# A four-layer perceiver kernel on one core: layer 2's cross attention moved to float32r in two parts, and five joints reordered

## The reference

```python
x = x + _L2_xattn_ref(ctx_1024, _layernorm(x))   # softmax(h_dec @ h_enc^T) @ h_enc, one head, 256 features
x = x + _L2_attn_ref(_layernorm(x), ...)         # begins with rmsnorm(x, w), 16 heads of 64
x = x + _L1_ffn_ref(_layernorm(x), ...)          # 16 experts, top 2 by a gate, and a shared one
x = x + _L1_attn_ref(...)  # ... @ Wu + bu
x = x + _L3_attn_ref(...)  # ... @ Wout + bout
```

## Time and profile before

| | us |
|---|---|
| median of 3 runs (lowest, highest) | 2077.07 (2073.99, 2083.38) |
| profiled execution, time of the run | 2084.2 |
| its span, first to last instruction | 2082.9 |
| busy in the span: PE / weight loads | 1902.7 (91%) / 1193.7 |
| VectorE / ScalarE / Pool | 1357.7 (65%) / 1219.6 (59%) / 542.5 (26%) |
| chain that ended last: PE / VectorE / ScalarE | 67% / 21% / 7% |
| mean granted TensorE clock | 0.955 |

### The profile page before, as it was taken

The page is one execution under the profiler, slowest core; times in us unless marked ns, Lnnn a source line. Parts: engine busy times, 40 slices in busy tenths (PEclk is TensorE's granted clock), DMA queues, the critical chain, the costliest instruction groups (busy, mean ns, idle before and its releaser), DMA issues.

```text
span 2082.9 us, 36948 instructions
## 1 busy us (share of the span) xinstructions
PE 1902.7 (91%) x13683; PEld 1193.7 (57%) x13683; DVE 1357.7 (65%) x3230; ACT 1219.6 (59%) x2770; POOL 542.5 (26%) x697
## 2 busy tenths in 40 slices
PE   7999999998998899999999877898898799788998
PEld 4555555554565455555555556657556688564656
DVE  3776668883767577667796567531356898477383
ACT  3787778895435288778888452342155687164251
POOL 2111111122621111011100355200033466164151
PEclk9999999999999699999999788999999899999999
DMA  9777567760113677667761213333101242200110
GB/s 207 155 147 146 116 129 149 146 136 1 41 41 55 122 143 144 124 115 154 148 94 17 84 34 107 112 103 99 46 21 59 85 123 72 86 1 9 41 54 11
DMA packets 114225, 191.48 MB, mean 92 GB/s; under 512 B 17096, under 2 KB 67072, under 8 KB 107520
## 3 DMA queue, kind: packets, MB, share of 16 engines
q1 hardware_dynamic: 113056, 188.11, 41.2%
q10 hardware_dynamic: 992, 1.02, 0.2%
HBM read 135.20 MB, written 2.69 MB: 66 GB/s over the span
## 4 chain that ended last, share of the span: by engine, by line
PE 67%; DVE 21%; ACT 7%; issue 2%; DMA 1%; POOL 1%; SPq 0%; DVEq 0%; ACTq 0%; POOLq 0%
DVE WK L861 9%; PE PS L798 8%; PE PS L688 8%; PE PS L356 6%; PE PS L705 6%; PE PS L364 5%; PE PS L676 4%; PE PS L717 4%; PE PS L1886 3%; PE PS L1911 3%; PE PS L2319 3%; PE PS L465 2%; PE PS L2261 2%; PE PS L492 2%; PE PS L513 2%
## 5 line engine op out<-in xcount | busy, mean ns | idle before, releaser
L861 DVE TENSOR_REDUCE WK<-PS 128x1 f32<-128x1024 f32 x512 | 621.6, 1223 | 227.5 <-PE PS L688 163.1
L969 ACT ACTIVATE WK<-PS 128x512 f32<-128x512 f32 x840 | 464.5, 601 | 38.9 <-PE PS L688 24.4
L688 PEld LDWEIGHTS PS<-QSR,KSR 51*128 51x128 f32 x2048 | 251.5, 187 | 244.1 <-ACT WK L969 91.0
L688 PE MATMUL PS<-QSR,KSR 51*128 51x256 f32 x2048 | 379.5, 307 | 9.6 <-ACT WK L969 1.3
L676 PE MATMUL PS<-KSR,QSR 51*128 51x512 f32 x1024 | 371.4, 454 | 9.3 <-DVE WK L861 3.4
L798 PE MATMUL PS<-WK 128*32 128x256 f32 x2528 | 219.5, 394 | 0.6 <-ACT WK L953 0.5
L676 PEld LDWEIGHTS PS<-KSR,QSR 51*128 51x128 f32 x1024 | 186.4, 188 | 21.5 <-issue 13.4
L992 POOL TENSOR_TENSOR WK<-WK 128x512 fp32r<-128x512 f32 x62 | 79.3, 1279 | 442.5 <-ACT WK L930 230.7
L564 ACT ACTIVATE WK<-PS,WK 128x256 f32<-128x256 f32 (+1 forms) x320 | 140.6, 451 | 77.4 <-DVE WK L532 48.3
L590 POOL TENSOR_TENSOR WK<-WK 128x128 f32<-128x128 f32 (+1 forms) x128 | 64.9, 507 | 255.1 <-DVE WK L550 219.4
L594 POOL TENSOR_TENSOR WK<-WK 128x512 f32<-128x512 f32 x96 | 99.9, 1041 | 74.3 <-DVE WK L547 56.3
(11 more groups left out here) (360 smaller groups left out, 3548.0 us busy)
## 6 DMA issues: line engine op xcount, KB each, us to landing
KSR<-WK SPq DMA_DIRECT2D x381, 128.0 KB
WB<-in_ctxT SPq DMA_DIRECT2D x78, 512.0 KB, 5.0
WK<-in_ctxT SPq DMA_DIRECT2D x40, 512.0 KB, 4.1
WA<-in_ctxT SPq DMA_DIRECT2D x26, 512.0 KB, 5.2
WK<-in_ctx SPq DMA_DIRECT2D x8, 1024.0 KB, 6.0
WK<-in_ctx SPq DMA_DIRECT2D x16, 512.0 KB, 4.3
QSR<-scratch_q SPq DMA_DIRECT2D x48, 128.0 KB, 4.4
WB<-in_L3f_qkv SPq DMA_DIRECT2D x2, 1536.0 KB, 6.6
```

What stands on the lines that cost most here:

```text
L688: return pe.e.matmul(tile["S", L, s, i][:, j * 256:j * 256 + 256], KS[s % 4][HALF[i % 2], kt * 128:(kt + 1) * 128], QS[HALF[i % 2], g % 2, ...
L861: dv.e.tensor_reduce(mt[:, n:n + 1], tile["R", L, s, n].rearrange("p a b -> p (a b)"), AX, ALU.max).then_inc(*dv.at("R", L, s, n))
L969: ac.e.activation(PR[n % NPR], tile["S", L, s, i], ACT.Exp).then_inc(*ac.at("E", L, s, i))
```

## The change

**Layer 2's cross attention in float32r, two parts.** `ctxT` and `ctx` chunks come in units of 1024 columns, numbered `n` 0 to 31 (16 and 16). ScalarE rounds a unit into `CH2[n % 4]` (`high2_act`), Pool subtracts it from the unit in place (`low2_pool`), giving the low part (`CXR`). ScalarE rounds the two halves of the transposed input into `HH2`, and VectorE writes `HL2`. A score tile is 6 matmuls instead of 2 (float32 ones). In phase 2 ScalarE rounds all transposed blocks (`PH2`), VectorE writes the low part (`PL2`), and a block has 3 products. `expx` is in halves of 2048 columns: batch 0's stand between batch 1's chunks, and batch 1's between batch 0's steps. In batch 1, VectorE copies the scores of tile `q=1`. `CT2` has 5 buffers, `CN2` 6 of 512 rows. The first two units are rounded and subtracted at the end of layer 1. `rms_b` writes `XR` from `X` with a root of `var * (1 + eps) + 1e-5 * eps`, instead of statistics of `XN`.

**Joints.** The ranking of the experts is done for all four tiles at once, comparisons (`rank_compare`) ahead of expert 1 and the rest (`rank_weigh`) behind it. The two biases are added to `X` by Pool at the start of the self attention. `ln0b` takes its root from the variance directly, ahead of the other.

```diff
@@ l2x_pe
+                    h, l = view(CH2[n % 4], 0, 1024, 2, 512), view(low2(n), 0, 1024, 2, 512)
                     for q in range(2):
+                        m = slice((bb * 2 + q) * 128, (bb * 2 + q + 1) * 128)
+                        b = take(banks, ("s2", n, q), ((dv if bb and q else ac), "s2c", n, q))
                         settle(b)
+                        pe.wait_ge(ac, "c2h", n)
                         for k in range(2):
-                            i = pe.e.matmul(b.ap, HT[:, k, t * 128:(t + 1) * 128], CT2[n % 3][:, k, :], start=k == 0,
-                                            stop=k == 1)
+                            pe.e.matmul(b.ap, HH2[:, k, m], h[:, k, :], start=k == 0, stop=False)
+                            pe.e.matmul(b.ap, HL2[:, k, m], h[:, k, :], start=False, stop=False)
+                        pe.wait_ge(po, "c2l", n)
+                        for k in range(2):
+                            i = pe.e.matmul(b.ap, HH2[:, k, m], l[:, k, :], start=False, stop=k == 1)
...
+                                pe.e.matmul(y, PH2[n % 4][:, c], h[:, j, :], start=k == 0, stop=False)
+                                pe.e.matmul(y, PH2[n % 4][:, c], l[:, j, :], start=False, stop=False)
+                                i = pe.e.matmul(y, PL2[n % 4][:, c], h[:, j, :], start=False, stop=k == 31)
@@ new helpers
+        def high2_act(n):
+            a, sem, event = raw2(n)
+            ac.wait_ge(sem, event)
+            if n >= 20:
+                ac.wait_ge(pe, "c2", (n - 20) * 2 + 1)
+            elif n >= 4:
+                ac.wait_ge(pe, "s2", n - 4, 1)
+            ac.e.activation(CH2[n % 4], WK[:, a:a + 1024], ACT.Copy).then_inc(*ac.at("c2h", n))
...
+        def low2_pool(n):
+            a = raw2(n)[0]
+            po.wait_ge(ac, "c2h", n)
+            po.wait_ge(po)
+            po.e.tensor_tensor(low2(n), WK[:, a:a + 1024], CH2[n % 4].bitcast(F), ALU.subtract).then_inc(*po.at("c2l", n))
@@ l2x_act, phase 2
+                    for q in range(2):
+                        n = (bb * 8 + g) * 2 + q
+                        ac.wait_ge(pe, "p2", n, 3)
+                        if n >= 4:
+                            ac.wait_ge(pe, "c2", n - 4)
+                        ac.e.activation(PH2[n % 4], tile["p2", n], ACT.Copy).then_inc(*ac.at("p2", n))
+                    if bb * 8 + g + 19 < 32:
+                        high2_act(bb * 8 + g + 19)
+                    if bb == 0 and g in (1, 2, 4, 5):
+                        expx(1, g % 3 - 1, g // 3)
@@ l1f_dve
+                if i == 0:
+                    low_act(0)
+                    rank_compare()
+                if i == 1:
+                    low_act(1)
+                    rank_weigh()
@@ l1f_act, at its end
+            for n in range(2):
+                high2_act(n)
@@ l1a_pool
+            po.wait_ge(d_l1a)
+            for t in range(NT):
+                po.wait_ge(dv, ("a1", "ln"), t)
+                po.wait_ge(po)
+                po.e.tensor_tensor(X[:, t, :], X[:, t, :], bu, ALU.add).then_inc(*po.at("xb1"))
```

More of the change, by code:

```diff
@@ L228, in build @@
         d_exp = [dma(f"expert{i}") for i in range(11)]
-        d_ct2 = [dma(f"l2ct{i}") for i in range(3)]
-        d_cn2 = [dma(f"l2cn{i}") for i in range(3)]
+        d_ct2 = [dma(f"l2ct{i}") for i in range(5)]
+        d_cn2 = [dma(f"l2cn{i}") for i in range(6)]
         d_ct3 = [dma(f"l3ct{i}") for i in range(3)]
@@ L1744, in l1f_dve, with rank_compare @@
         def l1f_dve():
[L1745 to L1750 removed]
+            def rank_compare():
+                for t in range(NT):
+                    dv.wait_ge(ac, "gate", t)
                 dv.e.tensor_tensor(cmpA, gj, gi, ALU.is_equal).then_inc(*dv.at())
@@ L1849, in l1f_pool @@
             end(po, "l1f")
+            for n in range(2):
+                low2_pool(n)
         def l1f_sp():
@@ L1858, in l1f_sp @@
                 load_expert(i)
-            for n in range(3):
+            for n in range(5):
                 sp.e.dma_start(CT2[n], tiles(D["ctxT"][:, n * 512:(n + 1) * 512])).then_inc(*d_ct2[n].at(n))
-            for n in range(3):
-                sp.e.dma_start(CN2[n], tiles(D["ctx"][n * 1024:(n + 1) * 1024, :])).then_inc(*d_cn2[n].at(n))
+            for m in range(4):
+                load_cn2(m)
         S2 = [view(WK, 4096 * i, 4096) for i in range(4)]
-        CT2 = [view(WK, 16384 + 1024 * i, 1024, 2, 512) for i in range(3)]
@@ L1868, in build @@
-        CN2 = [view(WK, 19456 + 2048 * i, 2048, 8, 256) for i in range(3)]
-        PT2 = [view(WK, 25600 + 512 * i, 512) for i in range(4)]
-        mxs = WK[:, 27648:27712]
+        CT2 = [view(WK, a, 1024, 2, 512) for a in (16384, 17408, 18432, 23552, 24576)]
+        CN2 = [view(WK, 19456 + 1024 * i, 1024, 4, 256) for i in range(6)]
+        PH2 = [EAR[:, 512 * i:512 * i + 512] for i in range(4)]
+        PL2 = [EAR[:, 2048 + 512 * i:2560 + 512 * i] for i in range(4)]
+        HH2, HL2 = view(EAR, 4096, 1024, 2, 512), view(EAR, 5120, 1024, 2, 512)
@@ new lines, in build, with raw2, load_cn2, low2 @@
+        CH2 = [WAR[:, 1024 * i:1024 * i + 1024] for i in range(4)]
+        mxs = WK[:, 32768:32832]
+        def raw2(n):
+            if n < 16:
+                return (16384, 17408, 18432, 23552, 24576)[n % 5], d_ct2[n % 5], n
+            m = n - 16
+            return 19456 + m % 6 * 1024, d_cn2[m % 6], m
+        def load_cn2(m):
+            sp.e.dma_start(CN2[m % 6], tiles(D["ctx"][m * 512:(m + 1) * 512, :])).then_inc(*d_cn2[m % 6].at(m))
+        def low2(n):
+            a = raw2(n)[0] - 16384
+            return CXR[:, a:a + 1024]
@@ L1872, in l2x_pe @@
         def l2x_pe():
             after(pe, "l1f")
-            turn_pe("h2x", XN, (dv, "ln2x"), dv, ac)
-            pe.wait_ge(dv, "h2x", 0)
-            pe.wait_ge(ac, "h2x", 1)
+            for f in range(2):
+                b = take(banks, ("h2x", f), (dv, "h2x", f))
+                settle(b)
+                for t in range(NT):
+                    pe.wait_ge(dv, "ln2x", t)
+                    pe.e.transpose(b.ap[:, t * 128:(t + 1) * 128], XN[:, t, f * 128:(f + 1) * 128],
+                                   idf[:, :]).then_inc(*pe.at("h2x", "T", f, t))
@@ L1877, in l2x_pe @@
+            for f in range(2):
+                pe.wait_ge(dv, "h2x", f)
             for bb in range(2):
@@ L1922, in peak, with rms_b @@
                                        negate=True).then_inc(*dv.at("m2", bb, q))
+            def rms_b(t):
+                dv.wait_ge(ac, "rms2", "sd", t)
+                dv.e.reciprocal(rs[:, t:t + 1], rs[:, t:t + 1]).then_inc(*dv.at())
+                dv.wait_ge(dv)
+                dv.e.tensor_scalar(XR[:, t, :], X[:, t, :], mv[:, t, 0:1], rs[:, t:t + 1], ALU.subtract, ALU.mult).then_inc(
+                    *dv.at("rms2", t))
             after(dv, "l1f")
-            turn_dve("h2x", 0)
+            for f in range(2):
+                dv.wait_ge(ac, "h2x", "hi", f)
+                dv.e.tensor_tensor(HL2[:, f, :], tile["h2x", f], HH2[:, f, :].bitcast(F), ALU.subtract).then_inc(
+                    *dv.at("h2x", f))
             for bb in range(2):
@@ L1999, in l2x_sp @@
             sp.e.dma_start(sm[:, 8:10], D["L2a_w"]).then_inc(*d_l2a.at())
-            for n in range(3, 16):
-                sp.wait_ge(pe, "s2", n - 3, 1)
-                sp.e.dma_start(CT2[n % 3], tiles(D["ctxT"][:, n * 512:(n + 1) * 512])).then_inc(*d_ct2[n % 3].at(n))
-            for n in range(3, 8):
-                sp.wait_ge(pe, "c2", (2 * (n - 3) + 1) * 2 + 1)
-                sp.e.dma_start(CN2[n % 3], tiles(D["ctx"][n * 1024:(n + 1) * 1024, :])).then_inc(*d_cn2[n % 3].at(n))
+            for n in range(5, 16):
+                sp.wait_ge(pe, "s2", n - 5, 1)
+                sp.e.dma_start(CT2[n % 5], tiles(D["ctxT"][:, n * 512:(n + 1) * 512])).then_inc(*d_ct2[n % 5].at(n))
+            for m in range(4, 16):
+                if m < 6:
+                    sp.wait_ge(pe, "s2", m + 9, 1)
+                else:
+                    sp.wait_ge(pe, "c2", (m - 6) * 2 + 1)
+                load_cn2(m)
+        EPS2 = float(np.finfo(np.float32).eps)
         L2A, a0 = [], 0
@@ L2612, in l3a_pool @@
                                            ALU.mult).then_inc(*po.at("rope3", l))
+            po.wait_ge(d_l3a)
+            for t in range(NT):
+                po.wait_ge(dv, ("a3", "ln"), t)
+                po.wait_ge(po)
+                po.e.tensor_tensor(X[:, t, :], X[:, t, :], ob3, ALU.add).then_inc(*po.at("xb3"))
             attn_pool(A3)
```

196 lines of the change are left out of this document (88 added, 108 removed).

## The result

| | kernel before | changed kernel |
|---|---|---|
| median of the runs on one chip, us (lowest to highest) | 2080.23 (2073.99 to 2096.3) | 2052.36 (2048.77 to 2055.27) |
| ratio to before, with its 95% interval | | 0.9849 [0.9814, 0.9884] |
| span of the profiled execution | 2082.9 | 2047.4 |
| mean granted clock | 0.955 | 0.959 |

The changed kernel is faster, by about 1.5%. The profiled executions lie 35.5 us apart, where the sum of terms said 37.7. The same kernel was measured twice more: 2044.47 us, ratio 0.9825 [0.9779, 0.9871], span 2045.0; and 2046.99 us, 0.9817 [0.9775, 0.9859], span 2049.0.

A forecast was written before the change was run, and what follows sets the result against it. PE was taken to bound layer 2's cross attention, VectorE alone the joints; terms of 26.0 us inside the stage, -2.9, +4.0, +6, +2.0, +1.8 and +0.8 sum to 37.7, giving 2039 us, range 2026 to 2057.

The forecast's parts named there:

- Scores, 11.6: Layer 2's cross attention scores: 192 float32r instructions at 0.228 us, 45.6 us against 57.2, gain 11.6 us.
- Products and the joint of the batches, 14.4 in sum: Layer 2's products gain 9.3 us, less 2.0 for the first wait and 1.4 for slips; the batches' joint gains 8.5.
- The lock and the split input, -2.9: Start of layer 2's scores: a VectorE tensor_scalar waits out Pool's subtraction, 2.2 us; splitting the transposed input adds 0.7.
- End of the stage, 4.0: End of layer 2's cross attention: 7.25 us falls to 3.2, the second norm's variance coming from the first's; gain 4.0.
- Ranking, 6: Layer 1's experts: comparisons before expert 1, the rest behind it, shorten PE's idle; gain 6 us, bounds 4 and 10.
- Layer 1's end, 2.0: Layer 1's self attention: bias additions leave VectorE's chain, but Pool's splits catch the tensor_scalars; gain 2.0 us (0 to 4).
- Layer 3, 1.8: Layer 3: four bias additions of 0.42 us plus gaps leave VectorE's chain, Pool being free; gain 1.8 us.
- Layer 0, 0.8: Layer 0, root to first normalised tile: one root, two small products and a round trip less; gain 0.8 us.
- Lock everywhere: Rival: each joint waits out a whole Pool operation, ranking and bias gain 2 instead of 8; time 2051 us, 15%.
- ScalarE or Pool as the bound: Rival: ScalarE's roundings or Pool's subtractions, not PE, bound layer 2; time 2042 to 2047 us, say 2045, 15%.
- Fewer meetings: Rival: no lock at the start of layer 2, ranking gains 10, the batches' joint 9.5; time 2031 us, 10%.
- Lower clock level over the stage: Rival: layer 2 runs at 1.2 GHz, 105 us more if throughout; over half of it, 2092 us; 3%.

The follow-up runs named there:

- split_f32: The kernel before with only batch 1's exponentials halved inside batch 0's steps and their maxima found ahead, products left in float32: ratio 0.9934.
- low_late: The changed kernel with Pool's second subtraction for layer 2 waiting until VectorE has normalised the last tile: 2041.28 us, ratio 0.9813.
- rank_old: The changed kernel with the old ranking, tile by tile between the experts' elements: 2055.1 us, ratio 0.9836.
- all_late: The changed kernel with Pool's second layer 2 subtraction and its later expert operand splits waiting for VectorE's normalizations and ranking: 2039.27 us, ratio 0.976.
- r_after: The changed kernel measured and profiled once more, with no edit: 2044.47 us, ratio 0.9825.
- two_products: The changed kernel with the third product left out, except for one matmul per score tile: 2031.14 us, ratio 0.9761.
- exp_late: The changed kernel with batch 1's four half exponentials put back behind batch 0's steps: 2048.15 us, ratio 0.985.

## Why the prediction was right

The mechanism was right nearly everywhere. The total fell in the range with some luck: three medians, 2052, 2044 and 2047, all lie above 2039, and by the first alone the rival at 2051 would look better. What decides against that rival is the terms.

- **Scores, 11.6: measured 11.1.** The instruction of 512 columns was taken from the expert loop, and stood the same, 0.228. The 0.5 is the clock: 0.94 in the stage, 0.96 assumed.
- **Products and the joint of the batches, 14.4 in sum: measured 15.7.** By parts: the first batch gained 2.0 where 4.65 less 3.4 for the first wait and the slips was forecast, the second 5.0 where it was 4.65, the joint 8.75 (12.0 to 3.25) where it was 8.5. The first product waits 1.40 us, not 2.0. The mis-sized term was left out rather than wrong: that the idle of 12 us also cost 1.3 us of lower clock behind it, which split_f32 showed and the earlier trace rows had on its last line, 4.74 against 3.46. Without it the arithmetic gave the second batch 3.9 (33.1 in split_f32 to 29.2), not 4.65: here two misses partly cancel. The prediction also named ScalarE alone as the cause of the joint, and the description of the kernel before has the maxima joined after each batch's chunks; for the second batch VectorE's order stood ahead of ScalarE's (7.79 us of idle, above).
- **The lock and the split input, -2.9: measured -2.3.** The place was right: Pool's second subtraction caught the first of four normalizations, 2.2 us behind the last expert's addition in both kernels (1331.08 was that one before, 1320.15 is now). The size was 0.6 too high: the operation ends with Pool's, so what it loses is its 2.02 less the 0.41 that it needs, 1.6, where the whole wait of 2.2 was charged. low_late removed 1.7 us of the joint, and 0.6 was left for the split.
- **End of the stage, 4.0: measured 4.4.** From 9.6 to 5.2.
- **Ranking, 6: measured 5.6 and 6.0** (rank_old). PE's idle time there was forecast at 2 to 6 us and is 1.71 + 4.04. Expert 1's last products come 7.3 us sooner behind the first product (1258.56 - 1235.70 against 1271.12 - 1240.97), and 1.7 is given back on the lower level, the loss that the forecast kept for its lower bound. The meeting with Pool is real: all_late took another 3.3 us out of the stage, toward the bound of 10 that the forecast gave for no meeting.
- **Layer 1's end, 2.0: measured 2.0**, and for the stated reason: Pool's splits now caught the tensor_scalars (2.05 and 1.78 us), and all_late, without them, has 3.3 us more.
- **Layer 3, 1.8: measured 1.9** in every profile with that edit (212.4 against 214.3 us). **Layer 0, 0.8: 1.0 at the joint;** then PE stays on the lower level longer (eight matmuls in 6.52 us behind it, 5.70 before), and only 0.2 was left.
- **The sum.** These add up to 38.6. The first profile lost 4.4 in layer 3 to the clock and 2 behind layer 2 (r_after, above), and had won 3.1 more than the terms ahead of the first expert product, which no run explains: 35.5. r_after's profile is 37.9 below the kernel before's. By medians measured side by side the gain is 28, 41 and 36 us.
- **The rivals.** Lock everywhere (15%): it is there at every place that was named, but it costs 0.7 us at the batches' joint and not 4.8, because what stands there ends with the tail of a Pool operation, and the ranking still gained. ScalarE or Pool as the bound (15%): did not happen; two_products showed it 0.2 us a chunk away. Fewer meetings (10%): did not happen; the one at the start of layer 2 is there. Lower clock level over the stage (3%): did not happen; 1.00 in both batches. But the list of signs asked for 0.95 or more in the stage and called any stretch at the lower clock wrong, and the scores have 0.94 with 5.4 us at the lower level. That sign was drawn too sharply: the kernel before has such a start as well (0.96 over its longer scores).

## What to carry to other kernels

Take an instruction's price from the nearest loop that already runs it beside the same neighbours: the two matmul sizes came within 1%, and those scaled from other lengths within about 4%, though the read behind each exponential, 0.18 us, was forgotten. Before changing a stage's arithmetic, split off what only reorders it: 11 of the 31 us of this stage came from the place, the halving and the earlier maxima of four exponentials. Where VectorE is alone on the chain and Pool has work in reserve, let Pool wait for a point behind that chain: two waits, with no arithmetic changed, gave 6.4 us more by stages here, and a third wait 1.6.

## What the runs showed that was not expected

- The same instructions ran at a granted clock of 0.50 for 10 us in one execution of the changed kernel and at 0.97 in its two others; it costs 4.4 us, as much as several terms of this sum. The part from the first projection behind layer 2 took 602.2, 597.8 and 597.7 us in the changed kernel's three profiles and 595.4 with another order ahead (exp_late).
- An operation of 128x1 elements with two SBUF inputs meets Pool like a large one: 0.82 us at the joint instead of 0.15.
- Pool's two-operand subtraction sets the pace at 2.51 us for 1024 columns when they follow one another, though a single one reads 2.405.
